# A recurrent attention layer between two expert layers: the first chunk in another order, and x*sigmoid(x) as one ScalarE function

## The chip, the cores and the metric

The kernel runs on one core of one Trainium2 chip. The time is device time of one execution in microseconds (us); the time before is the median of 3 runs. Engines are named TensorE, VectorE, ScalarE and GpSimd in the text, and PE, DVE, ACT and POOL in the profile; PEld is TensorE's weight load, SP the queue that issues most transfers.

## The reference

The input is `hidden`, 8 x 1024 x 256 in float32. The same expert layer stands on both sides of the attention:

```
x = x + 0.5 * ffn(layernorm(x), ...)
x = x + attn(layernorm(x), ...)
x = x + 0.5 * ffn(layernorm(x), ...)
```

The change lies in `attn`, a memory that is trained while it is read. The sequence goes through it in 8 chunks of 128 tokens for all 8 batches (D = 64):

```
k, v, q = causal_conv4(hidden @ Wk.T), ... Wv ..., ... Wq ...
alpha = (sigmoid(hidden @ aW.T + ab) * 0.1).mean(-1)
eta   = (sigmoid(hidden @ eW.T + eb) * 0.9 + 0.05).mean(-1)
theta = (softplus(hidden @ tW.T + tb) * 0.1).mean(-1)
for each chunk:
    # W1, W2 are the state at the chunk's start
    g = grad of sum((silu(k @ W1.T) @ W2.T - v)**2) for each token, * 0.1, norm clipped to 1
    per token: S = eta*S - theta*g ;  W = (1 - alpha)*W + S
    h = silu(q @ W1_t.T) ;  out = h @ W2_t.T
out = rmsnorm(out @ Wo.T) * norm_g * (hidden @ gW.T + gb)
```

The two layers with x*sigmoid(x) are `silu(k @ W1.T)`, of which the gradient also needs the slope, and `silu(q @ W1_t.T)`.

## The kernel before

The program is a row of blocks, one behind the other: router and experts of the first layer, the attention (`memory_attention`, from line 900), router and experts of the second. Within a block each engine has a hand-written list of instructions and runs it in that order; semaphores (`wait_ge`, `then_inc`) tie the engines together. So what stands early in an engine's list holds up all that stands behind it.

In the attention everything of one chunk is done for all 8 batches at once, in tiles of 128 x 1024 or 128 x 512. The eight banks of PSUM are four pairs, `A`, `BB`, `C`, `DD` (line 996), and almost each product waits until the earlier content of its pair was read. The pieces of one chunk are these.

- Normalise x: VectorE's statistics (`moments_of`, line 1131), GpSimd's power (lines 1062 and 1068), ScalarE's `normalise_batches` (line 1432). Then TensorE turns x into `A` and `BB` (`turn_x`, line 1638), ScalarE copies it as `xT_high` (line 1424), VectorE makes `xT_low` (`split_turned`, line 1156). After the second half was turned ScalarE issues the transfer of the next chunk's x (line 1423).
- Projections in three products each (`passes`, lines 1643 to 1645): keys and values, queries, the rates alpha and eta, and the gates (`gates`, four pairs of batches, read by VectorE at line 1237).
- ScalarE's last tap (lines 1454, 1465) and VectorE's three taps (line 1163) of the convolutions.
- Four scans along the tokens on VectorE: `momentum_scans` (1199), `carry_scans` (1205), `memory_scans` (1217), `decay_scans` (1221).
- First layer, `hidden`: TensorE's product into `C` (line 1726), ScalarE's Sigmoid (line 1508), VectorE's product `hid = C * sig_h` (line 1270), TensorE's turn of it back into `C` (line 1733), ScalarE's copy (line 1513), TensorE's `residual` (line 1740). Beside it VectorE makes the slope in two passes (1275, 1277) and `dpre` (1282).
- Norms, theta (ScalarE's Abs, Exp and Ln, lines 1489 to 1493) and the scaled gradients (1302, 1304), the new state (1779), the second layer: product (1751, 1753), ScalarE's Sigmoid (1526), VectorE's product `hid2` (1309), TensorE's `second_scores` (1759).

The first chunk's front part (all up to `scores`, `key_norms` and `hidden`) is written out once, ahead of the steps. `step(c)` then does the second part of chunk c together with the front part of chunk c+1, interleaved by hand. `step(0)` begins on TensorE with

```
if not last:
    turn_x(c + 1, False)
hidden_turned(c)
if not first:
    outputs(c - 1, 1)
residual(c, par)
if not last:
    kv_projection(c + 1)
```

and `turn_x(1)` can begin once `P1` (line 1264) freed `A`; its second half waits for `KNORM` (line 1260). `unread_products` (line 1851) are matmuls whose result nobody reads; before, they stand only at the end of the attention.

## Time and profile before

| | us |
|---|---|
| median of 3 runs | 854.41 (850.83 to 855.55) |
| the profiled execution's own time | 863.48 |
| its span in the profile | 861.6 |
| mean granted TensorE clock in it | 0.901 of full |
| TensorE busy, share of the span | 84% |
| VectorE busy | 70% |
| ScalarE busy | 51% |
| GpSimd busy | 29% |

The attention takes the stretch from about 205 to 673 us of the span. Busy shares are means over stages with different limits. A row of the timeline gives start, duration, engine, line, operation, tile written and tiles read, count, and in brackets how long the engine was idle before and what ended that. The granted clock is given as a share: 1.00 is TensorE at 2.4 GHz, 0.50 at 1.2 GHz.

### The profile page before, as it was taken

What the parts mean: (1) busy time and instruction counts of PE and PEld (TensorE: products, weight loads), DVE (VectorE), ACT (ScalarE), POOL (GpSimd) and SP (SyncE); (2) the same over time, 40 slices, a digit from 0 to 9 for tenths busy, and PEclk for the clock granted to TensorE, in tenths of its full rate; (3) what the DMA queues carried; (4) which work ended last, traced back from release to release, by engine and by line L of the source; (5) the groups of instructions that cost most, each with busy time, mean ns of one, the idle gap of its engine ahead of it and who ended that gap; (6) DMA issues with size and microseconds to landing.
All of it is one profiled execution on the core that took longest, in us unless ns stands there. A gap on an engine that the chain in (4) does not pass through costs nothing. (4 is left out here: it accounts for less than half of the span.)

```text
span 861.6 us, 15519 instructions
## 1 busy us (share of the span) xinstructions
PE 721.4 (84%) x5689; PEld 632.9 (73%) x5689; DVE 605.4 (70%) x1311; ACT 436.1 (51%) x1034; POOL 249.9 (29%) x185
## 2 busy tenths in 40 slices
PE   4449799995767999999999999999878238899996
PEld 2238799994566878888788887878756127799996
DVE  1877577843485978798888987977763655787761
ACT  1525457540636565665866568565432504475550
POOL 0053511314221143250623506142232045413202
PEclk9769899997888989999898999999977659999999
DMA  9975624613101012040130303103030723616300
GB/s 335 409 276 168 251 63 164 194 24 129 49 0 50 2 49 99 2 147 2 51 99 22 125 2 99 51 1 99 1 97 2 244 78 111 207 52 226 115 13 31
DMA packets 57858, 89.19 MB, mean 104 GB/s; under 512 B 6592, under 2 KB 48704, under 8 KB 57664
## 3 DMA queue, kind: packets, MB, share of 16 engines
q1 hardware_dynamic: 45808, 70.18, 23.5%
q0 software_dynamic: 3840, 10.49, 3.6%
q10 hardware_dynamic: 8144, 7.61, 3.0%
q8 instruction: 46, 0.75, 0.4%
q14 instruction: 20, 0.16, 0.1%
HBM read 74.63 MB, written 22.02 MB: 112 GB/s over the span
## 5 line engine op out<-in xcount | busy, mean ns | idle before, releaser
L626 PE MATMUL ps<-moe_normedT_high,weights_high_up 128*128 128x320 f32 x256 | 85.3, 333 | 11.4 <-DVE moe_hidden_low L484 7.2
L484 DVE SCALAR_TENSOR_TENSOR moe_hidden_low<-ps,moe_hidden_high 128x256 fp32r<-128x256 f32 x128 | 54.0, 422 | 40.7 <-ACT moe_hidden_high L589 36.5
L628 PE MATMUL ps<-moe_normedT_high,weights_low_up 128*128 128x320 f32 x256 | 82.4, 322 | 0.0
L627 PE MATMUL ps<-moe_normedT_low,weights_high_up 128*128 128x320 f32 x256 | 82.4, 322 | 0.0
L626 PE MATMUL ps<-weights_high_down,moe_hidden_high 128*128 128x256 f32 x256 | 73.4, 287 | 0.8 <-issue 0.8
L1079 POOL TENSOR_TENSOR att_o_rs<-att_o_mean,minus_half 128x4 f32<-128x4 f32 x16 | 16.2, 1013 | 197.3 <-DVE att_o_mean L1323 197.3
L628 PE MATMUL ps<-weights_high_down,moe_hidden_low 128*128 128x256 f32 x256 | 71.5, 279 | 0.8 <-issue 0.8
L627 PE MATMUL ps<-weights_low_down,moe_hidden_high 128*128 128x256 f32 x256 | 71.4, 279 | 0.0
L626 PEld LDWEIGHTS ps<-moe_normedT_high,weights_high_up 128*128 128x128 f32 x256 | 51.2, 200 | 14.2 <-DVE moe_hidden_low L484 6.1
L567 ACT CAST weights_high_down<-weights_raw_down 128x256 fp32r<-128x256 f32 x96 | 35.0, 408 | 42.2 <-PE ps L628 27.7
L588 ACT ACTIVATE moe_shared<-ps 128x64 f32<-128x64 f32 x128 | 29.0, 227 | 51.3 <-PE ps L628 44.7
L627 PEld LDWEIGHTS ps<-moe_normedT_low,weights_high_up 128*128 128x128 f32 x256 | 51.3, 201 | 0.0
L628 PEld LDWEIGHTS ps<-moe_normedT_high,weights_low_up 128*128 128x128 f32 x256 | 51.1, 199 | 0.0
L626 PEld LDWEIGHTS ps<-weights_high_down,moe_hidden_high 128*128 128x128 f32 x256 | 48.0, 188 | 3.9 <-issue 3.9
L276 DVE TENSOR_TENSOR weights_low_down<-weights_raw_down,weights_high_down 128x256 fp32r<-128x256 f32 x128 | 49.6, 420 | 0.4 <-ACT weights_high_down L567 0.4
L589 ACT ACTIVATE moe_hidden_high<-ps 128x256 fp32r<-128x256 f32 x128 | 48.7, 381 | 0.0
L276 DVE TENSOR_TENSOR weights_low_up<-weights_raw_up,weights_high_up 128x256 fp32r<-128x256 f32 x128 | 47.6, 419 | 1.5 <-ACT weights_high_up L567 0.9
L627 PEld LDWEIGHTS ps<-weights_low_down,moe_hidden_high 128*128 128x128 f32 x256 | 48.0, 188 | 0.5 <-issue 0.5
L628 PEld LDWEIGHTS ps<-weights_high_down,moe_hidden_low 128*128 128x128 f32 x256 | 48.1, 188 | 0.2 <-issue 0.2
L1643 PE MATMUL ps<-att_w_high,att_xT_high 128*128 128x320 f32 x128 | 42.3, 330 | 5.7 <-ACT att_keep L1480 4.9
L492 DVE SCALAR_TENSOR_TENSOR weights_rows<-ps,moe_prob,weights_rows 128x256 f32<-128x256 f32 (+1 forms) x40 | 19.3, 483 | 36.9 <-PE ps L628 22.1
L1086 POOL TENSOR_TENSOR weights_rows<-weights_rows,att_GATES 128x1024 f32<-128x1024 f32 x15 | 35.9, 2395 | 26.0 <-DVE att_GATES L1330 26.0
(292 smaller groups left out, 2159.0 us busy)
## 6 DMA issues: line engine op xcount, KB each, us to landing
weights_raw_up<-in_w SPq DMA_DIRECT2D x16, 1024.0 KB
weights_raw_down<-in_w SPq DMA_DIRECT2D x16, 1024.0 KB
first_xt<-in_xT SPq DMA_DIRECT2D x8, 1024.0 KB, 7.9
weights_rows<-x SPq DMA_DIRECT2D x8, 1024.0 KB, 5.6
out_x<-weights_rows SPq DMA_DIRECT2D x8, 1024.0 KB, 4.4
weights_rows<-x ACTq DMA_DIRECT2D x7, 1024.0 KB, 5.5
weights_rows<-x SPq DMA_DIRECT2D x2, 512.0 KB, 4.4
weights_raw_up<-in_w_x SPq DMA_DIRECT2D x1, 704.0 KB
```

Of the source, the lines that this page charges most:

```text
L276: self.nc.vector.tensor_tensor(self.piece(self.low, u, f), self.piece(self.raw, u, f), self.piece(self.high, u, f).bitcast(F32), ALU.subtr ...
L484: v.scalar_tensor_tensor(hidden_low[i][:, f, :], ps[:, 2 + (KF * i + f) % 3, WHOLE[i]], 0.0, hidden_high[i][:, f, :].bitcast(F32), ALU.max ...
L492: v.scalar_tensor_tensor(r, ps[:, 6 + n % 2, 0:H], prob[:, tile:tile + 1], r, ALU.mult, ALU.add).then_inc(y_read, 1)
L567: s.copy(weights.piece(weights.high, u, f), weights.piece(weights.raw, u, f)).then_inc(weights.high_done[u], 1)
L588: s.activation(shared[i][:, f, :], src[:, SHARED[i]], ACT.Relu).then_inc(shared_done, 1)
L589: s.activation(hidden_high[i][:, f, :], src[:, WHOLE[i]], ACT.Relu).then_inc(relu_done, 1)
L626: mm(dst, high_l, high_r, start=start, stop=False)
L627: mm(dst, high_l, low_r, start=False, stop=False)
L628: return mm(dst, low_l, high_r, start=False, stop=stop)
L1079: g.tensor_tensor(o_rs[:, n], o_mean[:, n], t["minus_half"][:, n], ALU.pow).then_inc(o_rs_ready, 1)
L1086: g.tensor_tensor(x_res[:, n, :], x_res[:, n, :], GATES[par][:, n, 0:H], ALU.add).then_inc(x2_ready, 1)
L1643: mm(dst, high_l, high_r, start=start, stop=False)
```

## The change

Three things are changed, all in `memory_attention`.

1. The first chunk's front part has another order on TensorE, VectorE and ScalarE. The second half of x is normalised by VectorE (new semaphore `x_normed_late`) instead of ScalarE. Queries go to `C`, the rates to `DD` and `A`, and the gates to `BB, A, DD, BB` (`FIRST_GATES`). `hidden_turned`, the gradient squares and `residual` of chunk 0 move from `step(0)` to ahead of it, so ahead of `turn_x(1)`. The square of the keys gets a buffer of its own (`first_k_sq`).
2. Before x has arrived, TensorE makes 8 unread products, and 5 more behind the turn of the state.
3. Sigmoid goes: the first layer uses ScalarE's Silu for `hid` and a Tanh of half the argument, `bend`, from which VectorE makes twice the slope (the 0.5 is in `dpre`); the second layer uses Silu alone; the rates use Tanh of half the argument with changed constants. VectorE's products at lines 1270 and 1309 are gone in all 8 chunks. A Silu of one column stands first on ScalarE.

The core of the diff:

```diff
-    sig_h, hid, slope = sb("sig_h", [P, B, D]), sb("hid", [P, B, D]), sb("slope", [P, B, D])
+    bend, hid, slope = sb("bend", [P, B, D]), sb("hid", [P, B, D]), sb("slope", [P, B, D])
...
-    k_sq = dpre
+    k_sq, first_k_sq = dpre, grad_w1
...
+    FIRST_GATES = BB, A, DD, BB
...
+                dve.wait_ge(rstd_done, 2)
+                for b in range(HALF, B):
+                    v.tensor_scalar(x_norm[:, b, :], x_norm[:, b, :], moments[:, b, 0:1], rstd[:, b:b + 1], ALU.subtract,
+                                    ALU.mult).then_inc(x_normed_late, 1)
...
-            def hidden(c, first):
-                dve.wait_ge(sig_ready, c + 1)
-                if not first:
-                    dve.wait_ge(hid_m_ready, c)
-                v.tensor_tensor(hid[:], wide(C)[:, :, 0:D], sig_h[:], ALU.mult).then_inc(hid_ready, 1)
-
             def slope_of(c):
                 dve.wait_ge(hid_ready, c + 1)
-
-                v.scalar_tensor_tensor(slope[:], sig_h[:], 1.0, hid[:], ALU.subtract, ALU.mult).then_inc(tmp_ready, 1)
+                dve.wait_ge(bend_ready, c + 1)
+                v.scalar_tensor_tensor(slope[:], hid[:], 1.0, bend[:], ALU.subtract, ALU.mult).then_inc(tmp_ready, 1)
                 dve.wait_ge(tmp_ready, c + 1)
-                v.tensor_tensor(slope[:], sig_h[:], slope[:], ALU.subtract).then_inc(slope_ready, 1)
+                v.scalar_tensor_tensor(slope[:], hid[:], 1.0, slope[:], ALU.add, ALU.subtract).then_inc(slope_ready, 1)
...
-            def second_hidden(c, par):
-                dve.wait_ge(sig2_ready, c + 1)
-                v.tensor_tensor(hid2[:], wide(DD), sig_h2[:], ALU.mult).then_inc(hid2_ready, 1)
...
             def hidden(c, first):
                 act.wait_ge(pre_made, c + 1)
                 if not first:
                     act.wait_ge(slope_ready, c)
-                s.activation(sig_h[:], wide(C)[:, :, 0:D], ACT.Sigmoid).then_inc(sig_ready, 1)
+                    act.wait_ge(hid_m_ready, c)
+                s.activation(hid[:], wide(C)[:, :, 0:D], ACT.Silu).then_inc(hid_ready, 1)
+                s.activation(bend[:], wide(C)[:, :, 0:D], ACT.Tanh, scale=0.5).then_inc(bend_ready, 1)
...
-                s.activation(sig_h2[:], wide(DD), ACT.Sigmoid).then_inc(sig2_ready, 1)
+                s.activation(hid2[:], wide(DD), ACT.Silu).then_inc(hid2_ready, 1)
...
             def hidden_turned(c):
                 pe.wait_ge(consts, 16 * len(loads))
                 pe.wait_ge(hid_ready, c + 1)
+                pe.wait_ge(bend_ready, c + 1)
...
+            pe.wait_ge(rounded, 2)
+            unread_products(8, 0)
             pe.wait_ge(consts, 16 * len(loads))
             pe.wait_ge(folded, 7)
             turn_state(state[0])
+            unread_products(5, 1, DD)
             gram(0)
             turn_x(0, True)
...
             ae_projection(0, BB)
-            pe.wait_ge(kv_copied, 1)
-            q_projection(0, A)
-            rates(0)
-            gates(0, range(4))
-            keys(0, 0)
+            pe.wait_ge(gram_copied, 1)
+            q_projection(0, C)
+            rates(0, True)
+            gate_pair(0, 0, FIRST_GATES[0])
+            pe.wait_ge(eta_ready, 1)
+            gate_pair(0, 1, FIRST_GATES[1])
+            pe.wait_ge(q_copied, 1)
+            hidden(0, 0, True)
+            pe.wait_ge(keep_ready, 1)
+            gate_pair(0, 2, FIRST_GATES[2])
+            pe.wait_ge(gate_read, 1)
+            gate_pair(0, 3, FIRST_GATES[3])
+            keys(0, 0, True)
             queries(0, 0)
-            hidden(0, 0, True)
+            hidden_turned(0)
+            residual(0, 0)
             step(0, 0, True, False)
```

How the lists stand at two places (line numbers of the changed kernel are some 10 higher). The first is ScalarE in the first chunk, from the queries' last tap on. `weights_rows` is the next chunk's x, `att_keep` and `att_eta` are the rates, `att_theta_log` is theta, and ACT_TABLE_LOAD loads the table that the next function needs. Before:

```order
L1465 ACTIVATE weights_raw_up<-att_raw_q,att_conv_q 128x1024
L1432 ACTIVATE weights_rows<-weights_rows,att_shift,att_rstd 128x256 x8
...
L1480 ACTIVATE att_keep<-ps 128x8x127
...
L1483 ACTIVATE att_eta<-ps 128x8x127
L1502 ACTIVATE att_dpre<-ps 128x512
L1489 ACTIVATE att_theta_log<-att_GATES 128x512
L1491 ACT_TABLE_LOAD
...
L1493 ACT_TABLE_LOAD
...
L1508 ACT_TABLE_LOAD
L1508 ACTIVATE att_sig_h<-ps 128x512
L1424 CAST att_xT_high<-ps 128x2x512
```

With the change:

```order
L1465 ACTIVATE weights_raw_up<-att_raw_q,att_conv_q 128x1024
...
L1482 ACTIVATE att_keep<-ps 128x8x127
...
L1485 ACTIVATE att_eta<-ps 128x8x127
L1511 ACTIVATE att_hid<-ps 128x512
L1512 ACTIVATE att_bend<-ps 128x512
L1433 ACTIVATE weights_rows<-weights_rows,att_shift,att_rstd 128x256 x8
L1517 COPY weights_raw_down<-ps 64x1024
...
L1491 ACTIVATE att_theta_log<-att_GATES 128x512
L1493 ACT_TABLE_LOAD
...
L1495 ACT_TABLE_LOAD
...
L1504 ACTIVATE att_grad_w<-ps 128x512
L1425 CAST att_xT_high<-ps 128x2x512
```

The first layer's function moved from behind theta to ahead of the next chunk's normalisation, and lost its table load there (the load stands at the very start of the block now).

The second place is TensorE at the end of the first chunk's front part, from the turn of the keys to the first projection of chunk 1. Before:

```order
L1699 MATMUL ps<-ident,weights_raw_down 128x128 x8
L1704 MATMUL ps<-weights_raw_up,weights_raw_down 128x128 x8
L1726 MATMUL ps<-weights_raw_up,weights_raw_down 128x64 x8
L1638 MATMUL ps<-ident,weights_rows 128x128 x16
L1733 MATMUL ps<-ident,att_hid 64x128 x8
L1740 MATMUL ps<-att_read_w,weights_raw_down 128x128 x8
L1643 MATMUL ps<-att_xT_high,att_w_high 128x512
```

With the change:

```order
L1709 MATMUL ps<-ident,weights_raw_down 128x128 x8
L1714 MATMUL ps<-weights_raw_up,weights_raw_down 128x128 x8
L1744 MATMUL ps<-ident,att_hid 64x128 x8
L1751 MATMUL ps<-att_read_w,weights_raw_down 128x128 x8
L1648 MATMUL ps<-ident,weights_rows 128x128 x16
L1653 MATMUL ps<-att_xT_high,att_w_high 128x512
```

The turn of the hidden layer and `residual` now stand ahead of the turn of x, and the layer's product (L1726 before) went further up, between the gates.

## Rows read from the trace of the kernel before

**Rows 1.** Windows view: stretch, its length, busy us of PE, PEld, DVE, ACT, POOL, clock, DMA.

```profile
216.00:262.00 46.00, 32.65 (x174) 27.16 (x172) 29.08 (x42) 24.65 (x35) 8.55 (x7) 0.84 0.08 23
...
365.00:416.50 51.50, 48.72 (x416) 42.12 (x417) 43.97 (x71) 32.68 (x58) 18.11 (x12) 0.95 0.20 63
```

**Rows 2.** Waits in one loop step, 361 to 415 us: waiter <- releaser: total, times, longest.

```profile
PE ps L1638 <- DVE att_KNORM L1260: 1.6, 1, 1.6
...
PE ps L1733 <- DVE att_hid L1270: 0.9, 1, 0.9
```

**Rows 3.** Timeline of ACT in the first chunk: start, us, engine, line, operation [idle <- releaser].

```profile
209.88 1.05 ACT L1601 COPY att_idents<-ident 128x1024 f32<-128x1024 f32 x1 [19.27 <-PEq L352]
...
217.55 4.05 ACT L1432 ACTIVATE weights_rows<-weights_rows,att_shift,att_rstd 128x256 f32<-128x256 f32 x8
...
228.18 1.02 ACT L1447 COPY att_raw_kv<-ps 128x1024 f32<-128x1024 f32 x1 [3.07 <-PE ps L1645]
229.23 1.26 ACT L1454 ACTIVATE weights_raw_down<-att_raw_kv,att_conv_kv 128x1024 f32<-128x1024 f32 x1
...
257.49 0.62 ACT L1489 ACTIVATE att_theta_log<-att_GATES 128x512 f32<-128x512 f32 x1
258.13 1.28 ACT L1491 ACT_TABLE_LOAD   x1
259.43 0.64 ACT L1491 ACTIVATE att_theta_log<-att_theta_log 128x512 f32<-128x512 f32 x1
...
263.31 0.60 ACT L1508 ACTIVATE att_sig_h<-ps 128x512 f32<-128x512 f32 x1
```

**Rows 4.** Timeline of DVE in the first chunk.

```profile
229.17 2.71 DVE L1131 BATCH_NORM_STATS2 att_stats<-weights_rows 128x6 f32<-128x256 f32 x8 [2.80 <-DMA weights_rows<-x]
...
240.75 0.18 DVE L1190 COPY att_raw_q<-att_raw_q 128x24 f32<-128x24 f32 x1
243.05 2.29 DVE L1199 TENSOR_TENSOR_SCAN att_mom<-att_eta,att_idents 128x1024 f32<-128x1024 f32 x1 [2.12 <-ACT att_eta L1483]
...
247.69 1.56 DVE L1237 TENSOR_TENSOR att_GATES<-ps,att_b_gt 128x640 f32<-128x640 f32 x2
...
258.23 1.22 DVE L1264 TENSOR_TENSOR att_P<-ps,att_M 128x1024 f32<-128x1024 f32 x1
...
263.94 0.69 DVE L1270 TENSOR_TENSOR att_hid<-ps,att_sig_h 128x512 f32<-128x512 f32 x1 [4.50 <-ACT att_sig_h L1508]
```

**Rows 5.** Timeline of PE in the first chunk, the turns, `residual` and the next projection.

```profile
212.38 1.94 PE L1788 MATMUL ps<-ident,weights_raw_up 128*128 128x128 f32 x8 [9.60 <-POOL weights_raw_up L1056]
...
219.68 3.94 PE L1638 MATMUL ps<-ident,weights_rows 128*128 128x128 f32 x16 [2.65 <-ACT weights_rows L1432]
...
254.64 1.07 PE L1699 MATMUL ps<-ident,weights_raw_down 128*128 128x128 f32 x8 [2.28 <-DVE att_GATES L1237]
...
257.52 1.89 PE L1726 MATMUL ps<-weights_raw_up,weights_raw_down 64*128 64x64 f32 x16
259.59 1.94 PE L1638 MATMUL ps<-ident,weights_rows 128*128 128x128 f32 x16 [0.18 <-DVE att_P L1264]
264.78 1.89 PE L1733 MATMUL ps<-ident,att_hid 128*64 128x128 f32 x8 [3.25 <-DVE att_hid L1270]
267.77 3.73 PE L1740 MATMUL ps<-att_read_w,weights_raw_down 128*128 128x128 f32 x16 [1.10 <-ACT weights_raw_down L1513]
271.20 0.53 PE L1643 MATMUL ps<-att_xT_high,att_w_high 128*128 128x512 f32 x1
```

**Rows 6.** Windows of 1 us at the head of two steps: length, PE busy, PEclk, DMA.

```profile
312.00:313.00 1.00, 0.00 (x0) 0.64 0.00 0
...
364.00:365.00 1.00, 0.00 (x0) 1.00 0.00 0
```

**Rows 7.** Timeline of ACT and PE in the last step, the second layer.

```profile
645.27 1.02 ACT L1526 ACTIVATE att_hid<-ps 128x1024 f32<-128x1024 f32 x1 [6.28 <-PE ps L1753]
...
647.60 2.05 PE L1759 MATMUL ps<-att_hid,weights_raw_down 64*128 64x128 f32 x16 [1.38 <-DVE att_hid L1309]
```

130 lines of the change are left out of this document (71 added, 59 removed).

## Prediction

> **What bounds the kernel now.** I read the windows by stage first. The change touches only the attention. A loop step of it takes some 51.5 us, of which TensorE is busy 48.72, VectorE 43.97 and ScalarE 32.68; the first chunk's front part takes 46 us with TensorE busy for only 32.65 [rows 1]. So a loop step is TensorE's: work taken from VectorE is worth there only what TensorE waited for it. The first chunk has over 13 us of holes. The waits of one loop step say which holes a step has: 1.6 us in the turn of x, until VectorE's key norm, and 0.9 us ahead of the turn of the hidden layer, until VectorE's `hid` [rows 2]. The first is not touched: the key norm waits for ScalarE's theta and its table loads, which keep their order in the loop. Last I read the timelines of the first chunk, engine by engine.
>
> **First chunk, up to the taps.** Before, ScalarE starts to normalise x at 217.55, behind two copies for the state, takes 4.05 for eight batches, and copies the keys' projection at 228.18 [rows 3]. TensorE's turn of x took 3.94 for 16, that is at half clock; 16 took 1.94 later on at full clock [rows 5]. With the change TensorE starts 8 unread products when the block opens, about 209.9, as ScalarE's first row does [rows 3]. 512 columns at 1.2 GHz are 0.43 us, so they end at 213.3. The state's turn (1.94, [rows 5]) follows, one microsecond later than before, at 215.3; ScalarE's copy of it takes about 0.6. The gram's copy no longer stands ahead of x and ScalarE does four batches only (2.0), while VectorE does the other four; so x is normalised at 218.0. The turn of x takes 1.94 if the unread products have brought the clock up, else 3.94, and ends at 219.9 to 221.9. From the end of that turn to the keys' copy it was 228.18 - 223.62 = 4.6 us [rows 3, 5], which stays. The copy starts at 224.5 to 226.5; I take 225.0, since TensorE has then been at work almost without a break for 8 us. The last tap ended 1.02 + 1.26 later [rows 3], so VectorE's taps start at 227.3.
>
> **VectorE's list.** From here VectorE is the chain. The next chunk's statistics and both convolutions ran from 229.17 to 240.93, 11.8 us [rows 4]; the change only swaps their order, so they end at 239.1. The rates are ready by then: ScalarE no longer puts 4.05 us of normalisation [rows 3] ahead of them, which before made VectorE wait 2.12 for eta [rows 4]. Gates 1.56, momentum scan 2.29, gates 1.56 [rows 4]: 244.5. Two slope passes at 0.69, priced as another 128x512 pass [rows 4], and two scans at 2.29: VectorE reaches `dpre` at 250.4. There it needs `residual`, which now stands in front of the scores. TensorE gets the fourth gate pair back at 244.5 and then does keys and queries (2.9, from the start of the keys to that of L1726), the turn, ScalarE's copy (1.1, by the gap in front of L1740) and `residual` [rows 5]. Turn and `residual` are seen only at half clock, 1.89 and 3.73 [rows 5]; half of that is the bound below. All at full clock it is ready at 251.5, all at half at 256.8; if the clock falls in the pause ahead of the keys and comes back on the way, near 254. The rest of VectorE's list up to `P1` was, of the 16.4 us from 243.05 to 259.45, what is left without the passes counted, 6.4 [rows 4], and that includes the key norm and small waits; I take 5.2, and 0.7 for `dpre`. So `turn_x(1)` starts at 257.4, with the middle value at 259.9, at worst at 262.7. Turned at half clock (3.94), with the last copy (1.0) and the last split (1.2) behind it, TensorE reaches chunk 1's keys projection at 263.6, 266.1 or 268.9. Before, it was 271.20 [rows 5]: there the three theta loads stood ahead of the Sigmoid at 263.31 [rows 3], `hid` came at 263.94 [rows 4], TensorE idled 3.25 and 1.10 and did turn and `residual` at half clock [rows 5]. The gain at this point is 7.6, 5.1 or 2.3. I take 6.5, nearer to the first, because the pauses ahead of the keys are short. What comes after is TensorE's again, but it has idled during VectorE's last passes, so the 12 products that follow may run at 0.43 instead of about half of it, 2.5 us in all; I take 1.0 of that. **First chunk: 5.5 gained**, bounds 0 and 8.
>
> **Theta's table loads on that path.** ScalarE squares the keys behind theta's two loads, and the key norm waits for it. In the trace a load takes 1.28; the Abs before it ends at 258.11 and Exp starts at 259.43 [rows 3], so a switch costs 1.3 and no more. By that theta, the squares and the keys' square end at 256.5, before `P1` is done, and cost nothing. The Trainium skill ("ScalarE: Activation LUTs", What ACT_TABLE_LOAD costs) puts a switch at 2.66 us, because a drain of 1.38 comes on top; by that the key norm would come 2 us later, TensorE's second half of the turn 0.6 later, and the first chunk would gain 4.9. The trace does not agree, so my sum has 5.5. The count of loads hardly changes: three in each loop step as before, and one more in step 0, ahead of `hid2`, where ScalarE waited for TensorE anyway; cost 0. If that cover were gone it would be 1.3, once.
>
> **Loop steps.** Before, TensorE's turn started 0.87 after the Sigmoid's end (263.91 to 264.78, [rows 3, 5]): VectorE's 0.69 and two hand-overs. Now it waits for Silu and Tanh; a 128x512 function takes 0.60 [rows 3], so it starts about 0.6 after Silu's end, 0.3 earlier. That can be had only where TensorE waits there; where the turn of x runs at half clock, it is itself later than `hid`. Seven times 0.3 is the upper bound, 2.1, nothing the lower; I take **1.0**. ScalarE copies x 0.5 later, but the projection that needs it starts five microseconds after the turn, and VectorE lost 0.69 there: cost 0. `hid2` without VectorE's pass gains nothing in the loop: TensorE has the turn of the state, the rates and the gram to do meanwhile, and VectorE waits next for eta, which ScalarE and TensorE set. The product with 0.5 in `dpre` and the second slope pass are the same size as before: 0.
>
> **Last step.** There nothing covers the second layer. ScalarE's Sigmoid runs from 645.27 to 646.29, and TensorE waits 1.38 until VectorE's product is done, to 647.60 [rows 7]. TensorE now starts at about 646.35: 1.25, and 0.25 for the first layer: **1.5**, bounds 1.2 and 2.
>
> **Sum.** 5.5 + 1.0 + 1.5 = 8.0 us. The profiled execution took 863.48 (span 861.6) and would take 855.5; against the median of 854.41, which is 1% lower, the forecast is **846.4**. Runs of this kernel differ by some 0.5%, 4.3 us, which is what I call no change.
>
> **Rivals.** *The hand-over eats it.* VectorE's list is longer by slope and `dpre` and TensorE runs it at half clock: the worst values above give 0 for the first chunk, 2.5 in all, 851.9. For it: the granted clock fell to 0.64 within a microsecond of idling in one step; against it: in another step it stayed at 1.00 through the same microsecond [rows 6]. Chance 0.13. *The clock holds in the steps.* A loop step has a granted clock of 0.95 [rows 1]: 5.2 us at half clock, 2.6 us lost. If the shorter wait spares half the steps that, 9 us more go: 837.4. Against it: the 1.6 us hole, which comes first, stays. Chance 0.11. *ScalarE becomes what TensorE waits for.* No row shows Silu or Tanh; I price them as Sigmoid. Let one cost e more per 128x512. TensorE's wait at the head of each step grows by 2e, in eight chunks, and by e in the last step: 17e. From e = 0.47 the whole gain is gone. With e = 0.6, a second pass over the tile, it is 10.2, and each step's head then surely falls to half clock, by the 2.6 above up to 6 us more in all: 862.6, slower. Against it: every other function and copy on that tile size takes about 0.6. Chance 0.03. The Trainium skill ("ScalarE: Activation LUTs", Rules for kernel authors) says that products belong on VectorE, not on ScalarE, and this change moves two of them the other way; by that rule this rival would be the likely one. By the rows the extra function costs less than VectorE's pass and its hand-over. *It does not do what it says*, as unread products that bring no clock: that is the upper value of the turn above, 2.0 us, and inside the range; chance of its own 0.01.
>
> **How the numbers follow.** The forecast has 0.72, with 839 to 850 as its own range: first chunk 0 to 8, loop 0 to 4 with the clock's luck, last step 1.2 to 2, and 2 for the median of three runs. The range reaches to the worst hand-over and to half of the clock's gain: 838.5 to 851.0. Faster by over 0.5%: 0.72 + 0.11 = 0.83; within 0.5%: 0.13 + 0.01 = 0.14; slower: 0.03.
>
> **What would show it.** Right: the keys' copy of chunk 0 at about 225; `turn_x(1)` near 257 and chunk 1's first projection near 264; its `residual` behind the queries at under 2.1 us; no idle time of VectorE from the first tap on but at `dpre`; Silu and Tanh at 0.60 and `hid2` at 1.02; in the last step TensorE's second scores under 0.1 behind Silu. Wrong: a VectorE wait at `dpre` of over 4 us, TensorE at 0.5 in chunk 1's projections, a longer wait ahead of the turn of the hidden layer than 0.9, or loop steps that differ from before by more than 1 us each.

## Result and profile after

The changed kernel takes **843.25 us** (median of 4, 838.8 to 846.02) against 853.02 for the kernel before beside it (4 runs, 850.83 to 855.55): ratio **0.9864, 95% interval 0.9821 to 0.9906**. The forecast was 846.4, with 838.5 to 851.0 as its range. Ratios here and below use a kernel's fast runs, which leaves out two of the seven of e3 (858.88 and 859.68), one of the kernel before (869.55) and one of e12 (1781.63). The profiled execution took 846.02 us (span 844.2, mean clock 0.907), 17.4 less in its span than the 861.6 of before.

Not all of that belongs to the change. I cut both spans at the attention's opening (ScalarE's first row of it, 209.88 [rows 3] and now 205.84), at the first layer's function (Sigmoid or Silu) of step 1 and of step 7, and at the router, which ends the attention. The first fence is the windows view of the kernel before; columns as in [rows 1]: stretch, length, busy time of PE, PEld, DVE, ACT, POOL, granted clock, DMA.

```profile
209.88:313.45 103.57, 81.09 (x546) 69.71 (x547) 73.92 (x131) 56.86 (x84) 25.63 (x19) 0.86 0.11 35
313.45:623.77 310.32, 297.49 (x2524) 257.39 (x2522) 260.52 (x406) 194.72 (x335) 107.39 (x64) 0.95 0.19 59
623.77:673.51 49.74, 35.91 (x287) 28.79 (x287) 22.61 (x41) 14.47 (x37) 12.42 (x7) 0.77 0.20 64
673.51:861.60 188.09, 146.00 (x1092) 134.86 (x1092) 122.01 (x351) 82.92 (x285) 50.96 (x45) 0.87 0.35 118
```

The same four stretches of the changed kernel:

```profile
205.84:302.82 96.98, 81.08 (x561) 69.09 (x562) 73.91 (x136) 56.68 (x83) 25.57 (x18) 0.91 0.12 37
302.82:611.49 308.67, 296.62 (x2522) 257.69 (x2520) 248.98 (x395) 197.06 (x341) 107.38 (x64) 0.94 0.19 59
611.49:658.12 46.63, 33.86 (x287) 27.33 (x287) 20.25 (x37) 14.96 (x38) 12.09 (x7) 0.82 0.22 68
658.12:844.20 186.08, 147.17 (x1092) 136.56 (x1092) 122.01 (x351) 82.99 (x285) 51.41 (x45) 0.86 0.35 119
```

The attention took 463.63 and takes 452.28: **11.35 us less**, of which 6.6 up to step 1, 1.65 in the loop and 3.1 in the last step. The other 6.0 are not the change's: 4.04 ahead of the attention and 2.01 behind it, in code that it does not touch. The same kernel profiled once more (e9 below) opened the attention at 201.7, another 4.1 us earlier. Among all the kernels of this study, which share that code, the attention opened anywhere from 201.7 to 212.2 us, and the router's part took 178.7 to 188.2. VectorE's passes in the loop fell by 11.5 us of work (260.52 to 248.98), and the loop by 1.65: what VectorE is spared there is hardly on the path.

From here on places in the first chunk are given as us behind the attention's opening, written +N. TensorE of the changed kernel there (compare [rows 5]):

```profile
205.88 3.44 PE L1865 MATMUL ps<-att_w_high 128*128 128x512 f32 x8 [7.11 <-PEq L352]
209.16 1.03 PE L1799 MATMUL ps<-ident,weights_raw_up 128*128 128x128 f32 x8
...
212.97 1.97 PE L1648 MATMUL ps<-ident,weights_rows 128*128 128x128 f32 x16 [0.55 <-ACT weights_rows L1433]
...
238.91 1.06 PE L1709 MATMUL ps<-ident,weights_raw_down 128*128 128x128 f32 x8 [1.55 <-DVE att_GATES L1250]
...
244.04 2.05 PE L1751 MATMUL ps<-att_read_w,weights_raw_down 128*128 128x128 f32 x16 [1.10 <-ACT weights_raw_down L1517]
251.76 3.65 PE L1648 MATMUL ps<-ident,weights_rows 128*128 128x128 f32 x16 [5.67 <-DVE att_P L1277]
258.19 0.79 PE L1653 MATMUL ps<-att_xT_high,att_w_high 128*128 128x512 f32 x1 [2.78 <-DVE att_xT_low L1169]
...
263.46 0.39 PE L1653 MATMUL ps<-att_xT_high,att_w_high 128*128 128x512 f32 x1
```

The granted clock is 0.50 while the 8 unread products of L1865 run and 1.00 behind them: the state's turn takes 1.03 where it took 1.94, and the turn of x 1.97 where it took 3.94 [rows 5]. `residual` (L1751) runs at full clock too. Then TensorE waits 5.67 us for VectorE's P1, turns x of chunk 1 at half clock (3.65), and runs 12 products of chunk 1's projection at 0.43 us apart (258.19 to 263.46) before it is at 0.23. VectorE's list over the same stretch (compare [rows 4]):

```profile
221.91 3.93 DVE L1176 SCALAR_TENSOR_TENSOR weights_raw_down<-att_raw_kv,att_conv_kv,weights_raw_down 128x1024 f32<-128x1024 f32 x3 [4.22 <-ACT weights_raw_down L1454]
...
246.13 0.69 DVE L1289 SCALAR_TENSOR_TENSOR att_dpre<-ps,att_slope 128x512 f32<-128x512 f32 x1 [1.52 <-PE ps L1751]
...
250.40 1.21 DVE L1277 TENSOR_TENSOR att_P<-ps,att_M 128x1024 f32<-128x1024 f32 x1
...
254.83 1.23 DVE L1169 TENSOR_TENSOR att_xT_low<-ps,att_xT_high 128x1024 fp32r<-128x1024 f32 x1 [2.63 <-ACT att_xT_high L1425]
```

Between the taps and the split of x it waits in one place only, 1.52 us at `dpre`. ScalarE (compare [rows 3], the last row with [rows 7]):

```profile
220.63 1.25 ACT L1454 ACTIVATE weights_raw_down<-att_raw_kv,att_conv_kv 128x1024 f32<-128x1024 f32 x1
...
233.68 0.60 ACT L1511 ACTIVATE att_hid<-ps 128x512 f32<-128x512 f32 x1 [4.04 <-PE ps L1736]
234.18 0.59 ACT L1512 ACTIVATE att_bend<-ps 128x512 f32<-128x512 f32 x1
...
244.42 0.62 ACT L1491 ACTIVATE att_theta_log<-att_GATES 128x512 f32<-128x512 f32 x1
245.05 1.28 ACT L1493 ACT_TABLE_LOAD   x1
246.35 0.63 ACT L1493 ACTIVATE att_theta_log<-att_theta_log 128x512 f32<-128x512 f32 x1
...
633.82 1.02 ACT L1530 ACTIVATE att_hid<-ps 128x1024 f32<-128x1024 f32 x1 [5.77 <-PE ps L1764]
```

Silu and Tanh take 0.60 and 0.59, and Sigmoid took 0.60 [rows 3]. In the last step Silu ends at 634.84, and TensorE's second scores start 0.06 later, where it had waited 1.38 [rows 7]:

```profile
634.90 2.05 PE L1770 MATMUL ps<-att_hid,weights_raw_down 64*128 64x128 f32 x16
...
638.35 0.44 PE L1778 MATMUL ps<-att_hid_ab,att_state 128*64 128x128 f32 x4 [1.04 <-DVE att_hid L1321]
638.59 0.42 PE L1780 MATMUL ps<-att_hid,att_grad_w 128*64 128x128 f32 x4
```

The retrieval products of L1778 and L1780 follow each other at 0.22 to 0.24 us. Before, the same groups stood 0.43 to 0.45 apart:

```profile
651.06 0.70 PE L1767 MATMUL ps<-att_hid_ab,att_state 128*64 128x128 f32 x4 [1.04 <-DVE att_hid L1318]
651.51 0.67 PE L1769 MATMUL ps<-att_hid,att_grad_w 128*64 128x128 f32 x4
```

### The profile page after: what moved, and what is told of

Its sections match the earlier page's. It is cut to its first block and busy times, and to the rows that moved or that the text cites. A ratio compares the mean times of both kernels' runs of the same rounds, so it can differ in the third digit from the quotient of the medians.

```text
span 844.2 us, 15540 instructions
## 1 busy us (share of the span) xinstructions
PE 720.9 (85%) x5702; PEld 632.8 (75%) x5702; DVE 591.8 (70%) x1300; ACT 439.1 (52%) x1040; POOL 248.4 (29%) x184
## 5 line engine op out<-in xcount | busy, mean ns | idle before, releaser
L628 PEld LDWEIGHTS ps<-moe_normedT_high,weights_low_up 128*128 128x128 f32 x256 | 51.5, 201 | 0.0
L276 DVE TENSOR_TENSOR weights_low_down<-weights_raw_down,weights_high_down 128x256 fp32r<-128x256 f32 x128 | 49.3, 416 | 0.6 <-ACT weights_high_down L567 0.6
L1653 PE MATMUL ps<-att_xT_high,att_w_high 128*128 128x512 f32 x96 | 40.6, 422 | 4.3 <-DVE att_xT_low L1169 4.3
L1561 ACT ACTIVATE att_squares<-ps 128x256 f32<-128x256 f32 x64 | 23.7, 385 | 34.8 <-PE ps L1817 34.4
```

The source lines that it names most:

```text
L276: self.nc.vector.tensor_tensor(self.piece(self.low, u, f), self.piece(self.raw, u, f), self.piece(self.high, u, f).bitcast(F32), ALU.subtr ...
L628: return mm(dst, low_l, high_r, start=False, stop=stop)
L1561: s.activation(o_sq[:, b, :], o[:, b, :], ACT.Square, accum_out=o_sum[:, bb:bb + 1]).then_inc(o_squared, 1)
L1653: mm(dst, high_l, high_r, start=start, stop=False)
```

## The experiments

Twelve kernels ran, four on each of three chips. The kernel before took 863.43 us beside the first four, 854.49 beside the next four and 854.09 beside the last, so only ratios compare between groups; and since the untouched parts vary by ten microseconds, each profile is read inside the attention. The last four columns are from one profile of each kernel. Times in us; "to Silu 1" is from the opening to the first layer's function of step 1, "loop" from there to that of step 7, "last" from there to the router.

| kernel | ratio to before (95%) | attention | to Silu 1 | loop | last |
|---|---|---|---|---|---|
| before | 1 | 463.6 | 103.6 | 310.3 | 49.7 |
| the change | 0.9864 (0.9821 to 0.9906) | 452.3 | 97.0 | 308.7 | 46.6 |
| e9, the change again | 0.9862 (0.9813 to 0.9910) | 453.4 | 97.7 | 309.0 | 46.6 |
| e1, functions only | 0.9954 (0.9918 to 0.9991) | 456.5 | 104.0 | 305.9 | 46.6 |
| e2, order only | 0.9918 (0.9891 to 0.9945) | 457.4 | 97.6 | 310.1 | 49.7 |
| e3, no unread products | 0.9905 (0.9860 to 0.9951) | 450.1 | 97.3 | 305.9 | 46.9 |
| e4, decay scan late | 0.9867 (0.9835 to 0.9899) | 449.6 | 94.7 | 308.2 | 46.6 |
| e5, Tanh twice | 0.9900 (0.9867 to 0.9933) | 452.2 | 97.1 | 309.0 | 46.1 |
| e6, residual back in step 0 | 0.9806 (0.9762 to 0.9851) | 445.8 | 93.1 | 306.1 | 46.6 |
| e7, scores first | 0.9798 (0.9757 to 0.9840) | 445.5 | 91.5 | 307.4 | 46.6 |
| e8, second product back | 0.9868 (0.9835 to 0.9901) | 455.0 | 97.1 | 308.6 | 49.3 |
| e10, turn first | 0.9841 (0.9802 to 0.9880) | 446.1 | 91.2 | 308.3 | 46.6 |
| e11, gap filled | 0.9843 (0.9799 to 0.9888) | 451.2 | 90.1 | 314.8 | 46.3 |
| e12, e11 and hid_m early | 0.9822 (0.9787 to 0.9857) | 448.3 | 90.4 | 311.3 | 46.6 |

### The two halves of the change: e1 and e2

e1 is the kernel before with this (and VectorE's `hidden` and `second_hidden` gone, slope and `dpre` rewritten for Tanh, the rates from Tanh):

```diff
-                s.activation(sig_h[:], wide(C)[:, :, 0:D], ACT.Sigmoid).then_inc(sig_ready, 1)
+                s.activation(hid[:], wide(C)[:, :, 0:D], ACT.Silu).then_inc(hid_ready, 1)
+                s.activation(bend[:], wide(C)[:, :, 0:D], ACT.Tanh, scale=0.5).then_inc(bend_ready, 1)
...
-                s.activation(sig_h2[:], wide(DD), ACT.Sigmoid).then_inc(sig2_ready, 1)
+                s.activation(hid2[:], wide(DD), ACT.Silu).then_inc(hid2_ready, 1)
```

> The kernel before with only the functions changed: Silu and Tanh on ScalarE in both layers, the rates from Tanh; the first chunk keeps its old order, its old banks and no unread products. My theory: the two parts of the change are separate, and this one gives the loop (1.65 us between the Sigmoid or Silu of step 1 and that of step 7) and the last step (3.1 us, of which about 1.6 through the clock), and at most 0.5 in the first chunk: the attention, 463.6 us in the trace of before, takes about 458.5, some 5 us less. Silu of chunk 1 then starts some 103 us behind the block's opening, as the Sigmoid did before (103.6; 97.0 with the whole change). Rival 1, the functions help only together with the new order (it is the order that brings the clock into the steps): loop and last step as before, the attention at 463. Rival 2, ScalarE becomes what TensorE waits for, hidden in the whole change by the first chunk's gain: the attention over 464.

Measured: ratio 0.9954; 104.0 to Silu 1 (nothing gained there), loop 305.9 (4.4 less, more than the 1.65 expected), last step 46.6 (3.1 less, as with the whole change), attention 456.5. Both rivals fall, on one profile.

e2 is the changed kernel with these functions taken back (Sigmoid on ScalarE, VectorE's two products), the order kept:

> The whole change without its functions: the first chunk's new order, banks and unread products, but ScalarE computes Sigmoid and VectorE multiplies, in both layers, as before. My theory: the order gives what the first chunk gained, 6.6 us at the Sigmoid of chunk 1 less up to 0.7 for VectorE's product in the first chunk, and nothing in the loop or the last step: the Sigmoid of chunk 1 some 97.5 us behind the block's opening, 310 from there to step 7's, 49.5 from there to the router, the attention about 457.5. Rival 1, the steps gain through the clock that the order brings: 308.7 in the loop here too. Rival 2, the first chunk's gain rests on VectorE's spared product (its list is the chain): the Sigmoid of chunk 1 at 99 or later.

Measured: ratio 0.9918; 97.6 to the Sigmoid of step 1, loop 310.1, last 49.7, attention 457.4 against 457.5 expected. So the first chunk's gain is the order's alone, and the last step's is the functions' alone. The ratios add up within their intervals (0.3 to 0.4% either way): 0.46% and 0.82% make 1.28%, and the change gives 1.36%. In the attention of the profiles the parts make 7.1 + 6.2 = 13.3 us and the whole 11.35 or, in its second profile, 10.2; most of the difference lies in the loop, where the parts gain 4.6 and the whole 1.65.

TensorE's waits say where the loop differs. In the kernel before (waiter, releaser: total, times, longest, from step 1 to step 7):

```profile
PE ps L1829 <- DVE att_GATES L1330: 1.3, 3, 0.6
PE ps L1733 <- DVE att_hid L1270: 0.9, 1, 0.9
```

and in the changed kernel:

```profile
PE ps L1744 <- ACT att_bend L1512: 1.2, 2, 0.6
```

L1829 is the turn of a chunk's finished output, which waits for VectorE's gated output. That wait shows in both kernels with Sigmoid (1.3 and, in e2, 1.5 us) and in none of the twelve with Silu, e8 among them, where VectorE has the second layer's product again; so it went with the first layer's functions. The wait ahead of the turn of the hidden layer, which the prediction priced, is no smaller in total. What lies between these 1.3 to 1.5 us and e1's 4.4 is not shown: e1 and e2 have the same mean clock in the loop, 0.95, and loops that are 4.2 us apart.

### The change again: e9

> The whole change once more, on the chip and among the runs of the variants beside it. My theory: order and functions are separate and add up. The order alone came to 0.9918 of before and the functions alone to 0.9954, so together 0.987 is expected, as in the result. The loop's time differs from one execution to the next with the clock (308.7, 308.2 and 305.9 us between the Silu of step 1 and that of step 7 in three profiles with these functions): 305.5 to 309 here, and the part that does not hang on it as before: 97.0 us from the block's opening to Silu of chunk 1, 46.6 behind the Silu of step 7. Rival: what differs between those profiles is no luck but set by the order of the first chunk; then this profile shows 308.7 again, within 0.3.

Measured: 0.9862, loop 309.0, last 46.6, to Silu 1 97.7 (0.7 more than in the first profile, by the clock at its start). The rival's value was 308.7 within 0.3; 309.0 is 0.35 away, too near to refute it, and the rest of the record fits the rival as well: the two profiles of the same kernel nearly agree, while e3 and e6, which differ from it in the first chunk alone, show 305.9 and 306.1. Whether the first chunk sets the loop's time or chance does is open. Ten profiles with the functions (all but e11 and e12) have a loop of 305.9 to 309.0, 307.7 in the mean; the two without have 310.3 and 310.1. e11 and e12 have the functions too and took 314.8 and 311.3.

### The unread products: e3

```diff
-            unread_products(8, 0)
...
-            unread_products(5, 1, DD)
```

> The whole change without its 13 unread products. My theory: they bring the clock up before x arrives, so without them the turn of x runs at half clock (3.9 us instead of 2.0) and the keys' projection behind it in part; the keys' last tap on ScalarE, 14.8 us behind the block's opening with them, comes at 16.5 to 17.5, and since VectorE is the chain from there, all of it is paid: 1.7 to 2.7 us, the attention 454 to 455. Rival: the copy of the keys waits for the normalisation of x anyway, which starts as early; the last tap at 15 and no difference. Second rival: without them the state's turn is done earlier, ScalarE's copy too, and x is normalised earlier; then the last tap comes at 14.5.

TensorE of e3:

```profile
216.79 3.08 PE L1648 MATMUL ps<-ident,weights_rows 128*128 128x128 f32 x16
...
256.62 3.62 PE L1648 MATMUL ps<-ident,weights_rows 128*128 128x128 f32 x16 [5.67 <-DVE att_P L1277]
263.02 0.50 PE L1653 MATMUL ps<-att_xT_high,att_w_high 128*128 128x512 f32 x1 [2.78 <-DVE att_xT_low L1169]
```

It opens at 209.48. The turn of x takes 3.08: the clock came up in its midst, so the state's two turns ahead of it bring the clock up too, only later. The keys' last tap comes at +16.0 instead of +14.8, the turn of x of chunk 1 at +47.1 instead of +45.9 and the first projection at +53.5 instead of +52.4: VectorE is the chain, and all 1.2 us are carried along, less than the 1.7 to 2.7 expected; both rivals (no difference, or earlier) fall. Behind the projection's start only 8 products ran at half clock instead of 12, and at Silu 1 but 0.35 was left of it. The unread products are worth 1.2 us where they stand. That this reaches the kernel's time is not shown: the ratio is 0.9905 on runs of 846.1 to 855.9, and e3's attention in the profile, 450.1, is shorter than the change's, by its loop.

### What the turn of chunk 1 waits for: e4, e6, e7, e10

e4 moves one scan of VectorE into its idle time:

```diff
             residual(0)
-            decay_scans(0)
             ends(0, 0, True)
             keys(0, 0, True)
             scores(0)
             key_norms(0, 0, first_k_sq)
+            decay_scans(0)
```

> The whole change with one pass moved in VectorE's list of the first chunk: the decay scan stands behind the key norm instead of ahead of the copy of the ends. My theory: VectorE's list up to the scores' product P1 is the chain to the turn of x of chunk 1, which waited 5.67 us for P1, while VectorE idles 2.63 us behind the key norm; one pass of about 2.2 us moved into that idle time starts the turn 2.2 us earlier, and the first projection of chunk 1, 52.4 us behind the block's opening, comes at 50.1 or, where the split of x behind it is then late by the moved pass, at 50.8: the attention takes 450 to 450.7. Rival 1: the second half of the turn waits for the key norm and that for ScalarE's theta and its two table loads (done by about 250 us of the trace, a microsecond ahead of the norm), so only about 1 us is gained. Rival 2: the moved pass stands in front of the split of x and eats what the turn gained: no difference, 452.3.

Measured: first projection at +50.5, Silu 1 at +94.7 (2.3 earlier than in the change's first profile), attention 449.6. The projection is where the theory had it and the attention just under it, and ScalarE showed for the first time. VectorE of e4:

```profile
255.33 0.69 DVE L1273 TENSOR_REDUCE att_KNORM<-att_grad_w 128x8 f32<-128x512 f32 x1 [1.01 <-ACT att_grad_w L1504]
```

With P1 1.8 earlier (+42.8 instead of +44.6), the key norm waits 1.01 us for ScalarE's square of the keys, which stands behind theta's two table loads. In the change the loads are hidden, as the prediction had it; two microseconds of progress uncover them. (The second half of the turn waited but 0.29 for the key norm.)

e6 undoes one move of the change: slope, the turn of the hidden layer, `residual`, `dpre` and the gradient squares of chunk 0 stand in step 0 again.

```diff
-            hidden_turned(0)
-            residual(0, 0)
             step(0, 0, True, False)
...
                 if not last:
                     turn_x(c + 1, False)
+                hidden_turned(c)
                 if not first:
-                    hidden_turned(c)
                     outputs(c - 1, 1)
-                    residual(c, par)
+                residual(c, par)
```

> The whole change with one of its moves undone: slope, the turn of the hidden layer, residual, dpre and the gradient squares of chunk 0 stand in step 0 again, behind the turn of x of chunk 1, as before. My theory: the move filled TensorE's and ScalarE's waiting time with work that otherwise stands on the path behind the turn of x. Without it VectorE reaches P1 3.6 us earlier (two slope passes 1.4, dpre 0.7, its wait for residual 1.5), so the first projection of chunk 1 is not reached later by the full 6 us that turn, copy and residual take (half clock 1.9 and 3.7, copy 1.0), but by some 1 to 3 us: Silu of chunk 1 at 98 to 100 behind the block's opening instead of 97.0 and 97.7, ratio to before 0.988 to 0.990. Rival 1: it is a wash, since VectorE's list is the chain and carries the same passes in either order: 97 to 98. Rival 2: the residual ahead of the turn is most of the first chunk's gain: over 102.

Measured: ratio **0.9806**, Silu 1 at +93.1, attention 445.8. All three theories had the move as a gain or a wash; undoing it takes 6.5 to 7.6 us out of the attention (452.3 and 453.4), 3.9 of the 6.5 before Silu 1 and the rest in the loop, for which the record gives no cause. The first part is read step by step below; the ratio's interval (0.9762 to 0.9851) overlaps that of the change. TensorE of e6, which opens at 204.44:

```profile
247.11 3.65 PE L1644 MATMUL ps<-ident,weights_rows 128*128 128x128 f32 x16 [6.39 <-DVE att_P L1277]
250.55 1.81 PE L1740 MATMUL ps<-ident,att_hid 128*64 128x128 f32 x8
253.46 2.05 PE L1747 MATMUL ps<-att_read_w,weights_raw_down 128*128 128x128 f32 x16 [1.09 <-ACT weights_raw_down L1516]
255.26 0.49 PE L1649 MATMUL ps<-att_xT_high,att_w_high 128*128 128x512 f32 x1
```

P1 starts 3.25 us earlier (+41.3 instead of +44.6), because VectorE makes it before slope and `dpre` and without the wait for `residual`, and so the turn of x does. Behind that turn TensorE has to wait for the copy and split of x anyway; the turn of the hidden layer and `residual` fill this wait instead of coming on top, and while they run the clock comes up. The projection starts at +50.8 instead of +52.4 and runs all its products at 0.23 instead of 12 at 0.43: 1.5 and 2.4, together the 3.9 us by which the new state's first product comes earlier (+59.3 against +63.2), and Silu 1 (93.1 against 97.0).

e7 keeps the move and makes P1 before the carry scan, `dpre` and the decay scan; ScalarE squares the keys ahead of theta:

```diff
             memory_scans(0, True)
-            carry_scans(0, True)
-            residual(0)
-            decay_scans(0)
             ends(0, 0, True)
             keys(0, 0, True)
             scores(0)
             key_norms(0, 0, first_k_sq)
+            carry_scans(0, True)
+            residual(0)
+            decay_scans(0)
...
             hidden_turned(0, 0, True)
+            keys(0, True)
             thetas(0, 0, True)
             gradients(0)
-            keys(0, True)
```

> The whole change with VectorE's list of the first chunk in another order: behind the memory scan come the ends, the keys' product KM, the scores' product P1 and the key norm, and only then the carry scan, dpre and the decay scan; ScalarE squares the keys ahead of theta. My theory: the turn of x of chunk 1, which waited for P1 at 45.9 us behind the block's opening, then starts right behind the residual, at 40.3, at full clock (2.0 us); ScalarE copies it behind theta's loads and the gradient squares, about 44, and the first projection of chunk 1 comes at 47.5 to 48.5 instead of 52.4; TensorE idles 5 us ahead of it and runs it at half clock as now. The Silu of chunk 1 at 93 to 94 instead of 97.0. Rival 1: GpSimd's preparation, which needs the decay scan, then stands in front of the power for the gradient norms and gives 2 us back: 95 to 96. Rival 2: VectorE's work per chunk is the same, so what the projection gains is lost at the next convolution: 97.

Measured: ratio **0.9798**, the lowest of all, and 836.54 against 841.48 us of the change on the same chip, though the runs (834.2 to 841.6 and 838.4 to 848.4) overlap; attention 445.5, against 452.3 and 453.4. TensorE of e7, which opens at 204.56:

```profile
244.69 1.91 PE L1648 MATMUL ps<-ident,weights_rows 128*128 128x128 f32 x16
252.52 0.80 PE L1653 MATMUL ps<-att_xT_high,att_w_high 128*128 128x512 f32 x1 [5.92 <-DVE att_xT_low L1169]
```

The turn starts at +40.1 at full clock and the projection at +48.0, both as expected; Silu 1 at +91.5 is better than the 93 to 94 expected, since only 6 products ran at half clock. The rivals (95 to 96, and 97) fall.

e10 goes on: VectorE splits x ahead of `dpre` and the decay scan, ScalarE copies x between theta's Exp and Ln, and GpSimd takes the power ahead of its preparation.

```diff
                 if not last:
                     split_turned(c + 1)
+                if first:
+                    residual(c)
+                    decay_scans(c)
...
-            prep(0, True)
             hidden(0, 0, True)
+            gradient_norm(0)
+            prep(0, True)
```

> The whole change with a further order of the first chunk: VectorE does ends, KM, P1, key norm and carry scan, then splits the turned x of chunk 1, and only then dpre and the decay scan; ScalarE squares the keys, does Abs and Exp of theta, copies the turned x, and only then does Ln and the gradient squares; GpSimd takes the power of the gradient norms ahead of its preparation. My theory: every wait ahead of the projection of chunk 1 goes but the residual, so its first product comes at 45 to 46 us behind the block's opening (52.4 with the change as it is), and since GpSimd's power is not held up the Silu of chunk 1 comes at 90.5 to 92 instead of 97.0: the attention takes some 446, 5 to 6.5 us less, ratio to before 0.980 to 0.982. Rival 1: from there TensorE waits for the gradients, which VectorE now makes later than the projections need: Silu of chunk 1 at 93 to 94, no better than the simpler order with the scores first. Rival 2: the gain is lost in the first loop step: 97 at Silu, ratio 0.987.

Measured: first product at +45.3 and Silu 1 at +91.2, both as expected, attention 446.1 as expected; but that is no better than e7, and the ratio is 0.9841. It reached the projection 2.7 us before e7 did and the new state only 0.4 before (+57.3 against +57.7): 14 products at half clock instead of 6, 1.6 us, and a wait of 0.62 for GpSimd's late preparation, whose last product took 1.50 us instead of 1.06 beside a VectorE pass. The chain had passed on to other waits, which is what its first rival said, though not by the size that it gave.

### ScalarE's price: e5 and e8

```diff
+                s.activation(bend_too[:], wide(C)[:, :, 0:D], ACT.Tanh, scale=0.5)
                 s.activation(bend[:], wide(C)[:, :, 0:D], ACT.Tanh, scale=0.5).then_inc(bend_ready, 1)
```

> The whole change with the Tanh of the first layer computed twice in every chunk, the extra one between Silu and the Tanh that is used. It measures what ScalarE's time costs at a step's head, the point on which the slower rival of the prediction rests. My theory: TensorE's turn of the hidden layer waits for ScalarE only where the turn of x ahead of it ran at full clock, in about half the steps; an extra 0.5 us there delays it by 0.5 in those steps and in the last one, and by nothing where the turn of x was slow: 1.5 to 3 us in all, ratio to before 0.989 to 0.991. Rival 1, the rival's own price: every step waits, 8 times 0.5, and the steps' heads lose the clock: 4 to 8 us, ratio 0.992 to 0.996. Rival 2, ScalarE is not on the path at all: under 1 us, ratio 0.987.

TensorE's wait for the Tanh in e5's loop (waiter, releaser: total, times, longest):

```profile
PE ps L1746 <- ACT att_bend L1514: 2.8, 4, 1.1
```

In four of six step heads TensorE waits for the Tanh, 1.1 us at the longest, 2.8 in all; in the change it was two of six, 0.6 at the longest, 1.2 in all. The extra half microsecond is on the path in those steps, as the theory had it; in the other two no wait shows. Yet the loop took 309.0, as in e9. The timed ratio, 0.9900 against 0.9862, is in the theory's range, but the intervals overlap, and the part of e5's span that lies in the attention shows no loss. The price of ScalarE's time is small; its size is not settled. Rival 1's 4 to 8 us show in no profile.

e8 puts VectorE's product of the second layer back, on top of Silu, so the layer's result is another one and only the time is read:

```diff
-                s.activation(hid2[:], wide(DD), ACT.Silu).then_inc(hid2_ready, 1)
+                s.activation(sig_h2[:], wide(DD), ACT.Silu).then_inc(sig2_ready, 1)
...
+                v.tensor_tensor(hid2[:], wide(DD), sig_h2[:], ALU.mult).then_inc(hid2_ready, 1)
```

> The whole change with VectorE's product of the second layer put back: ScalarE computes Silu, VectorE multiplies once more, so hid2 is the layer's input times its Silu and the output is another one; the instructions and their sizes are those of the kernel before. My theory: it gains nothing in the loop, where TensorE has other work (308 to 309 us between the Silu of step 1 and that of step 7), and 1.3 in the last step; what the last step gained beyond that, 1.6 to 1.8, came through the clock, since TensorE's wait for hid2 shrank: from the Silu of step 7 to the router 49 to 49.7 us instead of 46.6. Ratio to before 0.988 to 0.990. Rival 1: the clock gain belongs to the first layer's functions: 47.9 to the router. Rival 2: VectorE's 1.2 us per chunk count in the loop too, 7 us: over 312.

Loop and last step of e8, windows view:

```profile
303.90:612.52 308.62, 297.96 (x2522) 258.77 (x2520) 256.21 (x401) 197.03 (x340) 107.39 (x64) 0.94 0.19 59
612.52:661.78 49.26, 35.27 (x287) 28.71 (x287) 21.47 (x38) 14.96 (x38) 12.08 (x7) 0.79 0.20 65
```

The loop is that of the change although VectorE works 7.2 us more in it (256.21 against 248.98), and the last step takes 49.3 instead of 46.6. So of the 3.1 us of the last step 2.6 are the second layer's: 1.3 that TensorE no longer waits, and as much through the clock (0.82 instead of 0.79), which no longer falls for the retrieval. The remaining 0.5 are the first layer's. The ratio, 0.9868, is no higher than the change's, though 1.6 to 2.7 us (0.2 to 0.3%) were to be seen; the interval is wider than that.

### The gap ahead of the projection: e11 and e12

```diff
                 if not last:
                     turn_x(c + 1, False)
-                if not first:
+                if first:
+                    unread_products(22, 1, DD)
+                else:
                     hidden_turned(c)
```

> The order with the scores first (e7), and 22 unread products of TensorE between the turn of x of chunk 1 and its first projection, where it idled 5.9 us. My theory: they take 22 x 0.22 = 4.8 us at full clock, end a microsecond ahead of the projection, and keep the clock up; six of its products ran at 0.43 instead of 0.23 us, so 1.2 us are gained there: the new state's first product at 56.5 behind the block's opening instead of 57.7, Silu of chunk 1 at 90.3 instead of 91.5, ratio to before 0.978 to 0.979. Rival 1: the clock falls all the same behind the last of them or in the midst (then they take up to 9.5 us): the projection 3 us later, Silu of chunk 1 at 94. Rival 2: VectorE's list sets the Silu of chunk 1, not TensorE's: 91.5, no difference.

TensorE of e11, which opens at 203.65:

```profile
245.41 5.27 PE L1865 MATMUL ps<-att_w_high 128*128 128x512 f32 x22
251.57 0.50 PE L1653 MATMUL ps<-att_xT_high,att_w_high 128*128 128x512 f32 x1 [0.89 <-DVE att_xT_low L1169]
```

The first chunk does what was expected: no product at half clock, the new state at +56.4, Silu 1 at +90.1. But the loop took 314.8, and the ratio is 0.9843, not 0.978. Two steps took 54.6 and 54.2 where the others take 51.5. The start of the first of these, windows of 4 us:

```profile
396.88:400.88 4.00, 2.66 (x13) 2.26 (x12) 2.20 (x4) 2.06 (x3) 2.35 (x1) 0.50 0.00 0
400.88:404.88 4.00, 4.00 (x19) 2.64 (x18) 2.00 (x3) 2.02 (x2) 0.00 (x0) 0.54 0.58 177
```

and the same step of e7:

```profile
398.44:402.44 4.00, 4.00 (x21) 3.56 (x19) 2.20 (x4) 2.77 (x4) 2.35 (x1) 0.54 0.04 10
402.44:406.44 4.00, 3.96 (x29) 3.33 (x29) 3.38 (x5) 3.33 (x12) 0.88 (x1) 1.00 0.78 248
```

Counted from Silu on, TensorE stays at half clock for nearly 8 us there instead of 4. It also stands still in the midst of the turn of x, between the two halves, which in e7 follow each other:

```profile
399.23 1.97 PE L1648 MATMUL ps<-ident,weights_rows 128*128 128x128 f32 x8 [1.34 <-issue]
```

"issue" says that the profile shows nothing that TensorE waited for; the key norm, which this half needs, had ended at 396.29. The other long step has the same pause, 1.39 us. Nothing of the step's program differs. The cause is open, but chance alone is unlikely: e12, which has the 22 products too, has such pauses in the same two steps (0.96 and 1.24 us; the steps took 52.5 and 53.8), and in the other twelve profiles no step of the loop takes over 52.2. The timed runs do not settle it. They spread from 833.9 to 846.1, and the profiled one, with its slow loop, took 835.66, the second fastest of the six, since the parts outside the attention were short in it.

e12 adds one exchange in GpSimd's list:

```diff
-            prep(0, True)
             hidden(0, 0, True)
+            prep(0, True)
```

> e11 with GpSimd's product hid_m of the first chunk ahead of its preparation. In e7 a pass of VectorE on 128x8 (n1) took 1.92 us and ended with GpSimd's hid_m; the same pass took 0.17 in the change. My theory: VectorE and GpSimd share something, so the small pass waited until hid_m was done; with hid_m done at 38.5 behind the block's opening nothing of GpSimd runs there, n1 takes 0.17, and the gradients are made 1.7 us earlier. TensorE is not waiting for them, and VectorE's convolution of chunk 1 starts earlier, at 57.4 instead of 59.1: Silu of chunk 1 up to 1 us earlier, 89.3 to 90.3. Rival: it was a wait for the sum ahead of it, not GpSimd; then n1 takes 1.9 here too. Second rival: hid_m, now beside the products KM and P1, slows these by as much: the turn of x of chunk 1 1 to 2 us later.

Measured: n1 takes 0.17, KM and P1 1.22 and 1.21 as ever, and VectorE starts the convolution of chunk 1 at +57.6 where e7 had +59.1. So the theory of the held-up pass holds and both its rivals fall. Silu 1 comes at +90.4 against e11's +90.1: VectorE's 1.5 us are not on the path. Its loop, 311.3, again has a long step, of 53.8.

## Why the prediction was right

The total held (846.4 against 843.25), and so did its placing, though in part by luck: first chunk 5.5 forecast and 6.6 measured, loop 1.0 and 1.65, last step 1.5 and 3.1. All three are too small, and the sum of 8.0 stands against 11.35 in the attention of the profiles and 9.8 between the medians. Step by step:

- **Up to the taps.** Forecast: the clock comes up with the unread products, keys' copy at +15.1, VectorE's taps at +17.4. Measured +13.7 and +16.1. Right in the mechanism, 1.3 us better in size: the state's turn already ran at full clock (1.03, priced at 1.94), and ScalarE started on x at +5.0. The upper value (no clock from them) is excluded by the rows above and by e3.
- **VectorE's list.** Forecast from the taps to `dpre` 23.1 us; measured 22.7, up to the end of the carry scan. The wait at `dpre` was 1.52, near the lowest of the three values (1.1, 3.6, 6.4), since TensorE stayed at full clock through the pauses. The 6.5 that I took at the projection lies between the lowest and the middle value and puts the turn of x at about +48.6 and the projection at +54.8; they came at +45.9 and +52.4, and the gain at the projection was 9.0. My signs of being right asked for the turn near +47.1 (257), which does not go with the 6.5.
- **Half clock in chunk 1's projection.** Forecast 1.0 of 2.5 given back; measured 12 products and 2.4 us, the whole of it. I had named TensorE at 0.5 in these products as a sign of being wrong, and it showed. The two errors, 2.5 too little and 1.4 too little, partly cancel: 9.0 less 2.4 is the measured 6.6. That 5.5 came so near is luck to that extent.
- **Theta's table loads.** Forecast: covered, a switch at 1.3. Abs ends at 245.04 and Exp starts at 246.35: right, the load's 1.28 and no more. By the 2.66 of the Trainium skill ("ScalarE: Activation LUTs", What ACT_TABLE_LOAD costs) Exp would have started at 247.7; the trace does not agree. e4 showed how thin the cover was.
- **Loop steps.** Forecast 1.0, with 2.1 as the bound. Measured 1.65 and, over ten profiles, 1.1 to 4.4 (mean 2.5 against the two without). The size held and the mechanism did not. I took one step's wait of 0.9 [rows 2] for that of every step; before, it shows in one of six, and in the change TensorE waits there twice, 1.2 in all. What went instead is the wait for VectorE's gated output, 1.3 to 1.5, which my sum had not looked at; what the loops gained beyond that is not explained. The rival *the clock holds in the steps* (0.11, 9 us more) was half right: e3's loop had a clock of 0.98 and took 305.9, but in no profile did the loop gain more than 4.4, and in e11 and e12 it lost 4.5 and 0.9. That `hid2` gains nothing in the loop is right, by e8.
- **Last step.** Forecast 1.25 for the second layer and 0.25 for the first; measured 2.6 and 0.5 (e8). The mechanism is right, with the scores 0.06 behind Silu. What I left out is that a wait of TensorE that goes may also take away the fall of the clock behind it: half of the gain.
- **The rivals.** *ScalarE becomes what TensorE waits for* needed a Silu and Tanh dearer by 0.47; they cost 0.60 and 0.59, and e5 found little to pay even for another 0.5. The Trainium skill's advice to keep products on VectorE ("ScalarE: Activation LUTs", Rules for kernel authors) would have kept the kernel before; by e1 and e8 the trace does not bear it out here, where Silu takes the 0.60 us of Sigmoid and TensorE waits for its result. *It does not do what it says* is out. *The hand-over eats it* was half right, and it was the step that I weighed worst: I asked whether moving `residual` ahead of the turn would cost all of the gain, at the lowest clock, and gave it 0.13. e6 shows that the move costs 3.9 us although the turn and `residual` run at full clock. The rest of the order gains 10.5 us at the new state, and this one move gives 3.9 of them back. I had taken it as part of the gain because TensorE idled 3.25 and 1.10 there before; e6 shows no wait where the 3.25 stood, so that went with the earlier Silu and not with the place of `residual`, and the 1.10, for ScalarE's copy, stands in both orders (1.10 and 1.09). The range of the prediction is not what its reasons give: the worst hand-over, 851.9, lies outside it, and half of the clock's gain would be 841.9.

The experiments found two orders that look better than the change: e7 (0.9798) and e6 (0.9806), each with one piece of the first chunk's order changed. Their first chunks are 5.5 and 3.9 us shorter in the profiles; the intervals of the ratios still overlap that of the change. The two together were not tried.

## What to carry to other kernels

Before moving work "into a gap", ask which gap it leaves. The turn and `residual` went ahead of the turn of x, where VectorE was the chain and carried their passes, and left TensorE idle for 2.8 us behind it, where they would have been free and would have kept the clock up. Cut a change into its moves and price each by itself against the order without it, also where the sum looks good. And where a wait of TensorE goes, look at what ran behind it at half clock: here that doubled the gain of the last step.
